# A new order for the memory stage of a decoder layer, with the residual adds of GpSimd moved into its retrieval loop

## The reference

```python
h = relu(y @ scorer_w1.T); scores = sigmoid(h @ scorer_w2.T)      # one score for each token
# the 50 tokens of a sequence with the highest scores, if above 0.5, fill the pool:
order = argsort(-scores)[:, :50]
pool  = (y[order] @ summ_w.T)                                     # (50, 64) for each sequence
mean_score = mean(scores); retrieve_mask = (mean_score > 0.3) & (counts > 0)
q = y @ q_w.T;  k = pool @ k_w.T;  v = pool @ v_w.T
attn = softmax(where(memory_mask, q @ k.T / 4, -1e9))
retrieved = attn @ v
gate = sigmoid(concatenate([y, retrieved]) @ gate_w.T)
y = y + gate * retrieved * retrieve_mask
return residual + y
```

## Time and profile before

| | us |
|---|---|
| median of 3 executions | 773.06 |
| lowest, highest | 769.77, 777.85 |
| the profiled execution, its own time | 773.11 |
| span of its profile | 771.2 |
| mean granted TensorE clock, share of full | 0.903 |
| busy: TensorE | 671.1 (87%) |
| busy: VectorE | 411.9 (53%) |
| busy: ScalarE | 279.2 (36%) |
| busy: GpSimd | 219.7 (28%) |

### The profile page before, as it was taken

One profiled execution on the slowest core, in us unless ns is written; L12 is line 12 of the kernel. 1 busy time (PEld: TensorE's weight loads), 2 busy tenths in 40 slices (PEclk: granted clock), 3 DMA queues, 4 the chain that ended last, 5 costly groups with the idle time before them and its releaser, 6 DMA issues.

```text
span 771.2 us, 13694 instructions
## 1 busy us (share of the span) xinstructions
PE 671.1 (87%) x4832; PEld 519.2 (67%) x4833; DVE 411.9 (53%) x949; ACT 279.2 (36%) x567; POOL 219.7 (28%) x228
## 2 busy tenths in 40 slices
PE   0999948999999778988985899999973999999996
PEld 0744424767767545756653688888852999999995
DVE  4589995665566355312533455565536454454441
ACT  0487851222222261111263355455441332332320
POOL 1900007667776363002210000100012133233221
PEclk9799977999999795777975899999985999999998
DMA  6000001121112075000006000000037011111110
GB/s 206 1 0 0 1 6 56 42 62 41 41 41 82 0 275 218 1 1 2 1 13 205 1 17 15 16 23 16 16 93 230 15 37 33 32 35 34 30 27 0
DMA packets 38364, 37.93 MB, mean 49 GB/s; under 512 B 6791, under 2 KB 34764, under 8 KB 38316
## 3 DMA queue, kind: packets, MB, share of 16 engines
q1 hardware_dynamic: 33036, 32.11, 12.7%
q0 software_dynamic: 2208, 5.14, 2.4%
q10 hardware_dynamic: 3072, 0.05, 0.2%
HBM read 26.79 MB, written 5.13 MB: 41 GB/s over the span
## 4 chain that ended last, share of the span: by engine, by line
PE 59%; issue 14%; DVE 14%; POOL 7%; ACT 3%; DMA 2%; POOLq 0%; SPq 0%; DVEq 0%; ACTq 0%
PE banks L2019 11%; PE banks L2030 10%; DVE arena L1002 5%; PE banks L1883 3%; PE banks L1793 3%; PE banks L1906 2%; POOL arena L433 2%; PE banks L1859 2%; PE banks L1911 2%; PE banks L1924 2%; DVE arena L1014 2%; PE banks L1733 2%; POOL arena L418 2%; PE banks L1920 2%; PE banks L1543 2%
## 5 line engine op out<-in xcount | busy, mean ns | idle before, releaser
L2030 PE MATMUL banks<-arena,prob_b 128*128 x368 | 83.1, 380 | 0.0
L2019 PE MATMUL banks<-ybuf 128*128 128x128 f32 x560 | 79.8, 278 | 0.0
L2019 PEld LDWEIGHTS banks<-ybuf 128*128 128x128 f32 x560 | 73.3, 195 | 1.1
L2030 PEld LDWEIGHTS banks<-arena,prob_b 128*128 128x128 f32 x368 | 68.3, 190 | 8.3
L1543 PE MATMUL banks<-featT,ybuf 128*128 128x512 f32 x160 | 71.6, 611 | 0.5 <-DVE dts L978 0.5
L900 ACT ACTIVATE prob_b<-banks,gate_w 128x128 f32<-128x128 f32 x92 | 26.2, 368 | 117.8 <-PE banks L2019 117.8
L1292 DVE TENSOR_REDUCE ybuf<-banks 128x12 f32<-128x1848 f32 (+1 forms) x32 | 46.1, 1442 | 25.2 <-PE banks L1883 25.2
L1543 PEld LDWEIGHTS banks<-featT,ybuf 128*128 128x128 f32 x160 | 31.4, 197 | 40.0 <-issue 39.7
L562 POOL DMA_INDIRECT out<-featT,dts x23 | 23.3, 1014 | 121.8 <-DVE featT L1476 121.8
L542 POOL TENSOR_TENSOR xres<-xres,ybuf 128x256 f32 x16 | 11.6, 724 | 154.9 <-DVE ybuf L1312 154.9
L1002 DVE SCALAR_TENSOR_TENSOR arena<-arena,conv_w 128x512 f32<-128x512 f32 x72 | 48.8, 740 | 7.8 <-ACT arena L611 7.8
(11 more groups left out here) (347 smaller groups left out, 1403.7 us busy)
## 6 DMA issues: line engine op xcount, KB each, us to landing
arena<-W1T SPq DMA_DIRECT2D x8, 1024.0 KB, 13.3
arena<-W2T SPq DMA_DIRECT2D x8, 1024.0 KB, 10.5
arena<-arena SPq DMA_DIRECT2D x16, 384.0 KB, 3.1
xres<-x SPq DMA_DIRECT2D x4, 512.0 KB, 5.5
x_rows<-xres SPq DMA_DIRECT2D x16, 128.0 KB, 2.2
ybuf<-attn_in_wT SPq DMA_DIRECT2D x1, 1288.0 KB, 11.4
featT<-b SPq DMA_DIRECT2D x8, 128.0 KB, 3.7
w_out<-attn_out_wT SPq DMA_DIRECT2D x1, 512.0 KB, 12.7
```

What stands on the lines that cost most here:

```text
L2019: m = pe.matmul(bank[2 * p + half][:, f * P:(f + 1) * P], w1_now[k][p][:, (4 * half + f) * P:(4 * half + f + 1) * P], xsT[:, p, k, :], sta ...
L2030: m = pe.matmul(bank[4 + p][:, 0:D], hidT[:, p, f, :], w2_of[:, ds(e * NFF + f, 1), :].rearrange("p a n -> p (a n)"), start=(f == 0), stop ...
```

## The change

Six things are done.

1. The products of the memory weights move from the ranking to the gap between the last projection and the scan's cumulative sum, on TensorE and ScalarE; their loads move to the start of the program on SP. `w_nat`, `w_sk`, `w_key`, `w_vgate`, `w_valT` change their places in SBUF, and `w_val` overwrites `w_valT`.
2. `greater` gets room for all eight tiles of a sequence, so that VectorE ranks sequence 0 without waiting for counts. The scores of sequence 1 are halved (`half_plus(1)`) in the middle of that ranking.
3. The keys of the cross-attention are interleaved with the counts of sequence 0 instead of sequence 1. The values of sequence 0 stand ahead of `select(0)`, those of sequence 1 behind `memory_sides(0)`, and the counts of sequence 1 behind them.
4. ScalarE's queue follows: `keep_memory` is split into `keep_pool` and `keep_sides`, and `exp_logits(0)` stands ahead of `keep_pool(1)`.
5. In the retrieval loop `head` runs two steps ahead and stands between `turn_attn` and `retrieve`.
6. GpSimd adds `y_tok` to `xres` in 8 pairs of tiles: four in front of the loop, and one behind each of its first four adds. The clearing of `ybuf` follows in step 4 of the loop.

```diff
@@ SyncE, behind the load of w_out
+            for dst, src in ((scorer_w1[:, :, :], a["scorer_w1T"].rearrange("(k p) n -> p k n", p=P)),
...
+                             (gate_w[:, :, :], a["gate_wT"].rearrange("(k p) n -> p k n", p=P))):
+                sp.dma_start(dst, src).then_inc(S("mem_w_loaded"), 16)
             sp.wait_ge(S("conv_done"), NX * NBLK)
@@ GpSimd
-            for t in range(NT):
-                pool.tensor_tensor(xres[:, t, :], xres[:, t, :], y_tok[:, t, :], ALU.add).then_inc(S("res_y_added"), 1)
...
+            AHEAD = 4
+            def add_y(n):
+                xv = xres[:, 2 * n:2 * n + 2, :].rearrange("p a d -> p (a d)")
+                pool.tensor_tensor(xv, xv, y_tok[:, 2 * n:2 * n + 2, :].rearrange("p a d -> p (a d)"), ALU.add).then_inc(S("res_y_added"), 1)
+            pool.wait_ge(S("onehot_ready"), B)
...
+            for n in range(AHEAD):
+                add_y(n)
             for n in range(NT // 2):
                 pool.wait_ge(S("upd_ready"), n + 1)
+                pool.wait_ge(S("res_y_added"), n + 1)
                 xv = xres[:, 2 * n:2 * n + 2, :].rearrange("p a d -> p (a d)")
                 pool.tensor_tensor(xv, xv, upd[:, n % 2, :], ALU.add).then_inc(S("x1_ready"), 1)
+                if n + AHEAD < NT // 2:
+                    add_y(n + AHEAD)
+                if n == 4:
...
+                    pool.memset(ybuf[:, NG * P:3 * NG * P], 0.0).then_inc(S("pads_zero"), 1)
@@ ScalarE, last two steps of the projections
                 for f in Z_AT[q]:
                     tanh_gate(blk, f)
+                if p == PAIRS * NBLK - 1:
+                    act.wait_ge(pe_once, at("nat_turned"))
+                    act.activation(w_nat[0:SD, :, :].rearrange("p a n -> p (a n)"), bank[2][0:SD, :], ACT.Copy).then_inc(act_once, reached("nat_kept"))
                 if p:
                     tanh_conv(p - 1)
+            act.wait_ge(pe_once, at("w_sk_mm"))
+            act.activation(w_sk[0:SD, :], bank[3][0:SD, 0:D], ACT.Copy).then_inc(act_once, reached("w_sk_kept"))
...
+            act.wait_ge(pe_once, at("w_key_mm"))
+            act.activation(w_key.rearrange("p k n -> p (k n)"), bank[6][:, :], ACT.Copy).then_inc(act_once, reached("w_key_kept"))
             tanh_conv(PAIRS * NBLK - 1)
+            act.wait_ge(pe_once, at("w_vgate_mm"))
...
+            act.activation(w_val.rearrange("p k n -> p (k n)"), bank[3][:, :], ACT.Copy).then_inc(act_once, reached("w_val_kept"))
@@ ScalarE, memory stage
+            for n in range(B * NG):
...
+            keep_values(0)
+            keep_pool(0)
+            keep_sides(0)
+            keep_values(1)
...
             exp_logits(0)
+            keep_pool(1)
+            keep_sides(1)
@@ VectorE
+            half_plus(0)
             dve.wait_ge(S("x_w_loaded"), 16 * 9)
             dve.tensor_scalar(mask_row[:, :], mask_i[:, :], 0.0, 4 * NEG, ALU.is_gt, ALU.mult).then_inc(dve_once, reached("mask_row_ready"))
+            score_cols(0)
+            for k in range(TB):
+                rank_tile(0, k)
+                if k == 3:
+                    half_plus(1)
+            place_tokens(0)
             score_cols(1)
+            for k in range(TB):
+                rank_tile(1, k)
             place_tokens(1)
@@ TensorE, memory stage
+            for k in range(TB):
+                keys_of(k)
+                rank_cols(0, k)
+                if k == 4:
+                    pe.wait_ge(act_once, at("bias_ready_2"))
+                    turn_scores(1)
+            values_of(0)
+            select(0)
+            mean_scores(1)
+            memory_sides(0)
+            values_of(1)
+            for k in range(TB):
+                rank_cols(1, k)
...
             head(0)
             select(1)
             memory_sides(1)
             pe.wait_ge(S("vals_ready"), B)
+            head(1)
             for n in range(NT // 2):
-                if n + 1 < NT // 2:
-                    head(n + 1)
                 turn_attn(n)
                 if n >= 6:
                     turn_rows2(2 * n - 12)
+                if n + 2 < NT // 2:
+                    head(n + 2)
                 retrieve(n)
                 if n >= 6:
                     turn_rows2(2 * n - 11)
```

More of the change, by code:

```diff
@@ L128, in build @@
         tanh_c = cut([4, BLK])
+        w_nat = cut([2, D])
+        w_sk = cut([D])
+        assert place[0] <= 2 * NE * KD * FF
         place[0] = work0
@@ L188, in build @@
         tail_ctx = cut([B, KD, P])
-        greater = cut([2, T // 2]).bitcast(BF16)
+        GREATER_AT = [sum(TB - m for m in range(k)) * P for k in range(TB + 1)]
+        greater = cut([GREATER_AT[TB] // 2]).bitcast(BF16)
         onehot = cut([NT, POOL])
@@ L1545, in _ @@
                 m.then_inc(S("proj_mm"), 1)
+            summ, q_nat = w_nat[0:SD, 0, :], w_nat[0:SD, 1, :]
+            pe.wait_ge(S("mem_w_loaded"), 16 * 8)
+            pe.wait_ge(S("raw_ready"), NX * NBLK)
+            for i, w in enumerate((summ_w, mem_q_w)):
+                for k in range(KD):
+                    m = pe.transpose(bank[2][0:SD, i * D + k * P:i * D + (k + 1) * P], w[:, k, :], ident[:, :])
+            m.then_inc(pe_once, reached("nat_turned"))
+            pe.wait_ge(act_once, at("nat_kept"))
+            pe.matmul(bank[3][0:SD, 0:D], mem_k_w[:, :], summ, start=True, stop=True).then_inc(pe_once, reached("w_sk_mm"))
+            for k in range(KD):
+                m = pe.matmul(bank[5][:, k * D:(k + 1) * D], mem_v_w[:, k * P:(k + 1) * P], summ, start=True, stop=True)
+            m.then_inc(pe_once, reached("w_valT_mm"))
+            pe.wait_ge(act_once, at("w_sk_kept"))
+            for k in range(KD):
+                m = pe.matmul(bank[6][:, k * D:(k + 1) * D], w_sk[0:SD, k * P:(k + 1) * P], q_nat, start=True, stop=True)
+            m.then_inc(pe_once, reached("w_key_mm"))
+            pe.wait_ge(act_once, at("w_valT_kept"))
+            for c in range(KD):
+                for k in range(KD):
+                    m = pe.matmul(bank[2][:, c * D:(c + 1) * D], w_valT[:, k, c * P:(c + 1) * P], gate_w[:, KD + k, :],
+                                  start=(k == 0), stop=(k == KD - 1))
+            m.then_inc(pe_once, reached("w_vgate_mm"))
+            for k in range(KD):
+                m = pe.matmul(bank[3][:, k * D:(k + 1) * D], summ[:, k * P:(k + 1) * P], mem_v_w[:, :], start=True, stop=True)
+            m.then_inc(pe_once, reached("w_val_mm"))
             pe.wait_ge(dve_once, at("dt_ready"))
@@ L1769, in keys_of, with values_of @@
                           ).then_inc(S("keys_mm"), 1)
[L1771 to L1777 removed]
+            def values_of(b):
                 if b:
@@ L1784, in _ @@
                     pe.matmul(dst[0:rows, 0:D], ones[0:1, 0:rows], vb_row[:, :], start=False, stop=True).then_inc(S(done), 1)
+            pe.wait_ge(S("x_w_loaded"), 16 * 9)
+            pe.wait_ge(pool_once, at("bias_rows_cleared_2"))
+            for n in range(2):
+                m = pe.transpose(bank[5][:, BIAS_AT + n * NG:BIAS_AT + (n + 1) * NG], bias_rows[:, n, :, :].rearrange("g h c -> g (h c)"), ident[0:NG, 0:NG])
+            m.then_inc(pe_once, reached("bias_turned"))
+            pe.wait_ge(S("pads_ready"), 3)
+            pe.wait_ge(dve_once, at("mask_row_ready"))
+            for k in range(TB):
[11 more added lines that the diff above has]
+                rank_cols(1, k)
             def head(n):
```

176 lines of the change are left out of this document (55 added, 121 removed).

## The result

The changed kernel takes 756.63 us in the median of 20 runs (751.84 to 765.04), the kernel before 774.37 us beside it (20 runs, 761.75 to 784.62). The ratio is 0.985, with a 95% interval of 0.9805 to 0.9895; it compares only the executions that lie within 1.5% of the fastest of their kernel, which here are those up to 773.1 us before and up to 761.4 after. By it some 8 to 15 us are gone, clear of no change, but under 2%; 24.2 were forecast. The profiled execution took 756.66 us (span 754.9), 7.8 above the forecast and just outside the range. The forecast was counted from 773.06, and the kernel before also has executions of 762, so a part of the distance between 24.2 and 8 to 15 lies in where it was counted from.

The account below looks back on a forecast made before the run. TensorE was taken as the bound, busy for 60.8 of the memory stage's 69.2 us. A stage gain of 24.7 less 0.5 lost in the loop made 24.2 off 773.06: 748.9 us, range 739 to 756.5.

Parts of the forecast that it names:

- the sum: Memory stage: TensorE's work in line from 288.3 adds up to 44.5 us against 69.2, a gain of 24.7.
- Turns, keys and counts of 0: Start of the memory stage: small turns 0.2, turn of scores 0.8, keys and counts 10.3 us at full clock.
- The row of 5.47 us for 32 loads: Profile row of 32 loads with 8 columns, taken as nearest to each `select` in the memory stage: 5.4 us.
- the bound of 3.4: Lower bound for each `select` in the memory stage: 32 loads of 0.106 us at full clock.
- Products hidden in the gap: Memory weights' products, 10.9 us, leave the stage for TensorE's idle 9.7 us before the scan; cost there taken as 0.
- Rival D: Convolution gap: moved products spill over at half clock, holding cumulative sum and exponentials, 4 us; 753; chance 0.07.
- The loop: Retrieval loop: steps of 4.9 instead of 5.28 us; new order worth nothing by itself, 0.5 us lost.
- the bound that the prediction named: Loop's end: 0 to 2.5 us lost if the clock falls a step earlier, `retrieve(6)` and a turn at half.
- GpSimd: Moved y adds: nothing waits for them, 0; VectorE's gain of 0 to 0.4 us taken as 0.
- rival C: Retrieval loop: GpSimd's adds collide with the softmax, 7 us at most, half of it likely; 752.5; chance 0.08.
- B: Memory stage: clock low for longer, selects at 7.0, values 1 at half clock; 5 to 7 us less gain, 755; chance 0.17.
- A: Memory stage: clock stays full through both selects and sides, 9 us more gain, 739.9; chance 0.20.

Follow-up runs that it names:

- e6: Changed kernel with one unneeded product of 256 fp32 columns added behind each of the eight key blocks: 746.27 us, ratio 0.973.
- e12: Changed kernel with two unneeded products of 50 columns each added behind each key block: 765.94 us in the median of 10 runs.
- e5: Changed kernel with the memory weights' products and ScalarE's six copies back in the memory stage, loads still early: 768.69 us, ratio 1.0005.
- e4: Changed kernel with the retrieval loop in its old order, head(n+1) ahead of turn_attn(n): 757.59 us, ratio 0.984.
- e3: Changed kernel with GpSimd's 16 single y adds put back in the ranking: 757.81 us, ratio 0.983.
- e7: Changed kernel with head(1) between select(1) and memory_sides(1), without the wait for the copied values ahead of the loop: 755.83 us, ratio 0.986.
- e11: Changed kernel with values 0 among the keys, head(1) ahead of memory_sides(1), GpSimd's first four y adds ahead of its counters: 746.73 us, ratio 0.974.
- e10: Changed kernel with the four products of values 0 one behind each of the first four key blocks: 750.89 us, ratio 0.977.

## Why the prediction was wrong

**The terms of the stage.** From 289.2 to 340.2 it took 51.0 us, where the sum had 44.5.

- Turns, keys and counts of 0: 11.3 forecast, 14.3 measured. This is the step that failed first: "keys and counts of sequence 0: 10.3 at full clock" was read from a stretch that held 1.00 to its end. There the clock had risen at 318.5, 0.7 us ahead of the first key; here it had been up since 279.2, and falls 6.9 us behind the start of the first key.
- Values 0: 3.3 forecast, 6.3 measured, at half clock behind the keys.
- `select(0)`, copy and sides: 10.9 forecast, 13.0 measured. The select began at half clock and so took 7.1.
- Values 1, counts 1 and `head(0)`: 7.2 forecast, 7.0 measured.
- `select(1)` and copy: 5.8 forecast, 4.1 measured. The row of 5.47 us for 32 loads was the wrong neighbour; the bound of 3.4 was nearer.
- Sides 1 and the copy of the values: 6.0 forecast, 6.4 measured.

The errors add up to +6.5. All of the large ones are the clock's. The runs show it: e6 takes the fall away and has keys at 1.00, values of 3.3 and a select of 3.8; e12, profiled once, puts thin products in the same places and has none of it.

**Products hidden in the gap.** Right, and to the tenth: the gap is 9.7 us as before. But the forecast valued them at 10.9; alone they are worth 11.7 to 14.5 (e5). Rival D is refuted.

**The loop.** `head(1)` ahead of it and six steps: 31.7 forecast, 34.0 measured. `head(1)` took 4.1 instead of 2.3 at half clock, and each step 5.0 instead of 4.9, by the 0.21 that TensorE waits for tanh, where 0.1 was put. That the new order gains nothing is right. The end of the loop cost 0.6, forecast 0.5, and it is the bound that the prediction named, half of `retrieve(6)` at half clock; with it the order may cost about 1 us (e4).

**GpSimd.** Right: no gain and no loss (e3). That VectorE is held beside an add, rival C's mechanism, does occur (1.0 against 0.26 us), but beside the loop's own add and by the new order of the loop, not by the y adds that the rival named, and it is hidden. The page "SBUF — State Buffer" of the Trainium skill (SBUF: two separate sides), which calls the shared ports an exclusive lock, agrees with the trace here: in one step of the changed loop the add runs from 355.61 to 356.88 us, and the subtraction, begun at 356.02, ends at 356.99.

**Not in the sum.** The rest is 1.9 us shorter in the profiles of every variant but e7 and e11. No term of the forecast covered it. The clock stood at 0.52 over the first 7 us of the query products before, and at 1.00 after; the two windows, before and then after, are

```profile
414.20:421.20 7.00, 5.99 (x20) 3.93 (x24) 0.00 (x0) 1.98 (x7) 0.00 (x0) 0.52 0.32 100
```

```profile
399.80:406.80 7.00, 4.25 (x40) 2.94 (x40) 1.44 (x1) 2.94 (x10) 0.00 (x0) 1.00 0.33 102
```

Together: stage -18.2, `head(1)` and loop +2.3, end +0.6, rest -1.9, a later start of the stage +0.9, which makes the 16.3 us between the spans.

**The rivals.** B names what happened, in the first half of the stage, and A's full clock came in `select(1)` alone; they had been set as alternatives for both halves. B's 755 lies 1.7 us below the measured time, in part by luck: the keys lost 3.0 where it put 1 or 2, values 0 lost 3.0, which no rival had priced, values 1 lost nothing where it put 1.6, and `select(1)` won 1.7 where it lost. The page "TensorE: Matmul & The Clock Gate" of the Trainium skill (Part 1, what's actually happening) says that activity releases the throttle. The trace doesn't agree, if activity is taken for busy time: TensorE was busy for 6.27 of 6.27 us and 7.42 of 7.42 us at 0.50.

**What stays open.** How long behind the start of the keys the clock falls differs between executions of one kernel (6.9 and 2.9 us), and no run was made to find out why. Nor was it separated whether the columns themselves count, or the share of weight loads beside them. The comparison of dense and thin filler rests on one profile of each, and one short run of e12 speaks against it. What keeps the clock low at the first query products of e7 and e11 wasn't followed up.

## What to carry to other kernels

A stretch of TensorE that is busy without a gap can still run at half clock when its products have few columns; a forecast for it has to be given at either clock, and a row that held full clock once proves it only for what stood ahead of it. Dense products that must be made anyway are worth trying strewn among thin ones rather than gathered in one piece: here that won 3.9 us of the stage (e10), little more than the 3 us between two executions. When the line gets shorter, look at once for the engine whose work was hidden beside it: GpSimd's counters cost nothing until TensorE came to the loop 7 us earlier.

## What the hardware did that was not expected

- Work added to the critical engine made the kernel faster: 8 x 0.53 us of unneeded products of 256 columns took 6.6 us off the stage (e6). Thin products in the same places made it 9.9 us longer (e12): 7 by their own time at half clock, the rest by a clock that fell earlier.
- With few columns the weight load sets the pace, and it follows the clock as well: 32 loads of `select` took 3.67 us at 1.00 (0.115 each) and 7.07 at 0.50 (0.22 each).
- The start of an execution isn't reproducible: the products of 8 columns ahead of the projections ran at 0.106 us a load in one profile and 0.214 in another of these kernels, and the projections begin up to 6 us apart for that. In the profile after they were slow while the granted clock's column still reads 1.00 (25 to 39 us), so what that column shows ahead of its first change isn't to be relied on.
- A two-input operation of VectorE on 100 columns took 1.0 us beside GpSimd's add of 1.27 us, against 0.26 alone.
